# An attention and mixture-of-experts block in float32: weight loads and stores on ScalarE's queue, a row buffer of its own for the last batch, and a first tile table of eight

## The reference

```python
h = _layernorm(x) * (1 + ca) + sa
q, k, v = (h @ w + b, split into 16 heads)
scores = einsum('bhnd,bhmd->bhnm', q, k) * dmask      # gamma**(n-m), n >= m
ret = einsum('bhnm,bhmv->bhnv', scores, v)
x = x + ga * ((silu(h @ wg + bg) * groupnorm(ret)) @ wo + bo)
h = _layernorm(x) * (1 + cb) + sb
logits = h @ gate_kernel                              # 8 experts, the best 2, softmax over the 2
inter = silu(h @ w0[e]) * (h @ w1[e])                 # 256 -> 512
x = x + gb * sum over the 2 experts (weight * inter @ wo[e])
```

## Time and profile before

| | us |
|---|---|
| median of the 3 timed executions (422.52 to 423.67) | 422.94 |
| the profiled execution, device time | 424.81 |
| its span, from the first to the last instruction | 423.1 |
| first part, until PE turns the first routed rows | about 172 |
| tiles 0 to 8 | about 78 |
| tiles 9 to 38 and the last writes | about 173 |

### The profile page before, as it was taken

One profiled execution on the slowest core, in us unless ns is written; L12 is line 12 of the kernel. 1 busy time (PEld: TensorE's weight loads), 2 busy tenths in 40 slices (PEclk: granted clock), 3 DMA queues, 4 the chain that ended last, 5 costly groups with the idle time before them and its releaser, 6 DMA issues.

```text
span 423.1 us, 11448 instructions
## 1 busy us (share of the span) xinstructions
PE 373.8 (88%) x3889; PEld 278.0 (66%) x3890; DVE 257.2 (61%) x726; ACT 171.5 (41%) x262; POOL 229.5 (54%) x172
## 2 busy tenths in 40 slices
PE   3995899999889859887799899999999999999990
PEld 3464657776666537654476468888888888888870
DVE  6368317836833658673265566777777777777740
ACT  3514145463444311221331145555555555555530
POOL 3202520563754253617256457787777778777751
PEclk9998589999968988999699999999999999999997
DMA  6819007007900884217229844433333433433322
GB/s 226 273 34 317 4 24 279 28 2 258 323 24 3 282 294 119 52 52 252 53 42 285 245 84 75 78 75 75 75 75 75 75 75 75 75 75 76 51 25 25
DMA packets 32322, 49.05 MB, mean 116 GB/s; under 512 B 3198, under 2 KB 18972, under 8 KB 32284
## 3 DMA queue, kind: packets, MB, share of 16 engines
q1 hardware_dynamic: 23656, 34.60, 27.4%
q0 software_dynamic: 8176, 13.65, 14.6%
q10 hardware_dynamic: 452, 0.28, 0.2%
HBM read 30.35 MB, written 18.16 MB: 115 GB/s over the span
## 4 chain that ended last, share of the span: by engine, by line
PE 67%; issue 8%; DVE 8%; ACT 4%; DMA 4%; POOL 3%; SPq 2%; POOLq 0%; ACTq 0%; DVEq 0%
PE ps L1686 14%; PE ps L1391 9%; PE ps L1670 6%; PE ps L1667 6%; PE ps L1666 6%; PE ps L1678 3%; PE ps L1505 3%; PE ps L1657 3%; PE ps L1410 3%; PE ps L1444 2%; PE ps L1480 2%; DMA out_dram<-wg_s,qd 2%; POOL routed L591 2%; PE ps L1573 2%; PE ps L1465 1%
## 5 line engine op out<-in xcount | busy, mean ns | idle before, releaser
L623 POOL TENSOR_TENSOR w_lo<-we,w_hi 128x1024 fp32r<-128x1024 f32 x30 | 74.7, 2490 | 20.7 <-ACT w_hi L807 20.5
L1686 PE MATMUL ps<-we,qeo 128*128 x312 | 77.7, 393 | 6.6 <-ACT qeo L792 6.2
L1686 PEld LDWEIGHTS ps<-we,qeo 128*128 128x128 f32 x312 | 58.2, 193 | 25.1 <-issue 17.7
L633 POOL DMA_INDIRECT out_dram<-wg_s,qd x30 | 47.1, 1570 | 38.8 <-issue 15.8
L792 ACT COPY qeo<-ps 128x512 f32<-128x512 f32 x39 | 22.9, 586 | 105.1 <-PE ps L1678 105.1
L591 POOL DMA_INDIRECT routed<-h,idx x32 | 33.0, 1031 | 20.1 <-DVE idx L1131 11.2
L1292 DVE TENSOR_TENSOR w_halves<-we,w_halves 128x1024 fp32r<-128x1024 f32 x30 | 36.8, 1226 | 7.6 <-ACT w_halves L807 7.6
L1657 PE MATMUL ps<-we,xn 128*128 x72 | 36.5, 632 | 0.8 <-issue 0.8
L1272 DVE SCALAR_TENSOR_TENSOR sm<-sm,ps 128x512 f32<-128x512 f32 x39 | 26.5, 679 | 12.7 <-ACT sm L797 12.7
L1264 DVE CAST rT_halves<-ps 128x256 fp32r<-128x256 f32 x30 | 12.7, 424 | 33.2 <-PE ps L1573 33.2
L807 ACT CAST w_hi<-we 128x1024 fp32r x30 | 31.6, 1053 | 0.0
(11 more groups left out here) (228 smaller groups left out, 725.2 us busy)
## 6 DMA issues: line engine op xcount, KB each, us to landing
rowbuf<-routed SPq DMA_DIRECT2D x39, 260.5 KB, 2.9
we<-in_ffn_w_kernel_dram SPq DMA_DIRECT2D x16, 512.0 KB
we<-in_ffn_wo_kernel_dram SPq DMA_DIRECT2D x8, 512.0 KB
routed<-z SPq DMA_DIRECT2D x9, 260.5 KB, 3.9
xs<-in_attn_x_dram SPq DMA_DIRECT2D x4, 512.0 KB, 11.7
out_dram<-xs SPq DMA_DIRECT2D x4, 512.0 KB, 3.1
we<-in_wmod_dram SPq DMA_DIRECT2D x1, 1024.0 KB, 10.0
sbcb<-gsc_dram SPq DMA_DIRECT2D x4, 256.0 KB, 5.8
```

The costliest lines, as they stand in the source:

```text
L623: g.tensor_tensor(w_lo[1], expert_up(e, 1), w_hi[1].bitcast(F32), ALU.subtract)\
L633: g.indirect_dma_start(out, bass.IndirectOffsetOnAxis(ap=meta[s % 4][:, TOK - D:TOK - D + 1].bitcast(I32), axis=0), ey[s % 2], None, compu ...
L1686: last = mm(down_ps, eit[s % 2][:, k, :], weights(e, 2 * FT * F + k * D, D), start=k == 0, stop=k == KF - 1)
```

## The change

1. `load_expert` moves from SP to ACT. Experts 0 and 1 are issued after `keys(0, 1)`. For b = 1 to 3, expert 2b is issued after `queries(b, 0)` and expert 2b + 1 after `keys(b, 0)`. They no longer wait for `pv_done`.
2. `store_x` moves from SP to ACT, behind `features(b + 1)`, and for batch 3 behind step 2.
3. Batch 3 gets a row buffer of its own, `h2_last`, in the memory of `vx` and the first 36 columns of `z`. `second_normed(3)` and the fill of gb lose their wait for the scatters. The high halves of w0 lie in `vx` too, so ACT waits for all scatters before it writes those of tile `EARLY`.
4. `EARLY` goes from 9 to 8. `turn_h2(3)`, the router, `rank` and the second table come one step sooner on PE, DVE, ACT and POOL.
5. In batch 3, `counts(0)` on PE comes behind the projection k1. On DVE `tiles_before(0)` comes behind `group_stats` and `tile_columns(0)` ahead of `gated`.

```diff
-EARLY = 9
+EARLY = 8
...
+        h2_last = nc.alloc_sbuf_tensor_at("h2_last", [P, NC, ROW], F32, offset=offset["vx"])
+        h2 = [h2_first, h2_first, h2_first, h2_last]
...
-                load_expert(2 * b)
-                load_expert(2 * b + 1)
...
                 if i == 1:
-                    store_x(B - 2, x2_out)
                     sp.wait_ge(h2_ready, B - 1)
                     load_sbcb(B - 1)
-                if i == 3:
-                    store_x(B - 1, x2_last)
-                if i == 4:
                     fill_gb(B - 1)
-                if i == 7:
+                if i == 6:
...
                 queries(b, 0)
+                if b == B - 1:
+                    act.wait_ge(gb_out, 16)
+                if b:
+                    load_expert(2 * b)
...
                 keys(b, 0)
+                if b:
+                    load_expert(2 * b + 1)
                 keys(b, 1)
+                if b == 0:
+                    load_expert(0)
+                    load_expert(1)
...
                 act.wait_ge(shift2, b + 1)
-                if b:
+                if 0 < b < B - 1:
                     act.wait_ge(scattered, SCATTERS * b)
...
                     act.wait_ge(we_in, 16 * 3 * E)
+                    act.wait_ge(scattered, SCATTERS * B)
...
             second_normed(b)
-            act_step(2, 2)
             h2_features(b, [0])
-            act_step(3, 3, between=lambda: h2_features(b, [1]))
+            act_step(2, 2, between=lambda: h2_features(b, [1]))
+            store_x(b)
...
                     if last:
                         tiles_of_experts(0)
-                        tiles_before(0)
                     group_stats(p)
+                    if last:
+                        tiles_before(0)
...
+                if last:
+                    tile_columns(0)
                 if p >= 0:
                     gated(p)
                 fr.wait()
-                if last:
-                    tile_columns(0)
                 states(b)
...
-            pe_step(2, 2)
-            pe_step(3, 3, between=lambda: turn_h2(b, [0]), before_second=lambda: turn_h2(b, [1]),
+            pe_step(2, 2, between=lambda: turn_h2(b, [0]), before_second=lambda: turn_h2(b, [1]),
                     before_down=lambda: router(b))
-            pe_step(4, 4, before_second=lambda: rank(b))
-            pe_step(5, 5, between=lambda: counts(1))
-            pe_step(6, 6, between=lambda: firsts(1))
-            pe_step(7, 7, between=lambda: fold(1))
+            pe_step(3, 3, before_second=lambda: rank(b))
+            pe_step(4, 4, between=lambda: counts(1))
+            pe_step(5, 5, between=lambda: firsts(1))
+            pe_step(6, 6, between=lambda: fold(1))
```

More of the change, by code:

```diff
@@ L412, in _ @@
             load_ga(1)
-            def store_x(b, done_sem):
-                wait(sp, tail.drains(b, "wo23"))
-                sp.dma_start(out_v[b], xs[:, b * NC:(b + 1) * NC, :]).then_inc(done_sem, 16)
             def fill_gb(b):
-                if b:
+                if b == B - 1:
+                    sp.wait_ge(pv_done, SETS * B)
+                elif b:
                     sp.wait_ge(scattered, SCATTERS * b)
-                sp.dma_start(h2[:, 0, GB:ROW], gb_dram[b].partition_broadcast(P)).then_inc(gb_rows, 16)
-            for b in range(B):
+                sp.dma_start(h2[b][:, 0, GB:ROW], gb_dram[b].partition_broadcast(P)).then_inc(gb_rows, 16)
+            for b in range(1, B):
                 p = b - 1
[L427 to L431, removed]
-                    sp.wait_ge(gb_out, 16)
-                load_expert(2 * b)
-                load_expert(2 * b + 1)
[L435 to L445, removed]
+                sp.wait_ge(pv_done, SETS * b)
+                if b + 1 < B:
+                    sp.wait_ge(x1_ready, b)
+                    load_ga(b + 1)
+                if p >= 1:
+                    sp.wait_ge(h2_ready, p)
+                    load_sbcb(p)
+                if p == 0:
+                    sp.wait_ge(gb_out, 16)
+                fill_gb(p)
             def load_rows(i, s):
@@ L591, in scatter @@
                         g.indirect_dma_start(routed, bass.IndirectOffsetOnAxis(ap=idx[:, k, t:t + 1], axis=0),
-                                             h2[:, t, :], None).then_inc(scattered, 16)
+                                             h2[b][:, t, :], None).then_inc(scattered, 16)
             pool.sem_inc(added_ok, 4)
@@ L740, in gb_copies, with load_expert, store_x @@
                 act.wait_ge(gb_rows, 16 * (b + 1))
-                a.copy(h2[:, 1:NC, GB:ROW], h2[:, 0:1, GB:ROW].broadcast_to([P, NC - 1, D])).then_inc(gb_copied, 1)
+                if b == B - 1:
+                    act.wait_ge(prod_ready, FT * B)
+                a.copy(h2[b][:, 1:NC, GB:ROW], h2[b][:, 0:1, GB:ROW].broadcast_to([P, NC - 1, D])).then_inc(gb_copied, 1)
+            def load_expert(e):
+                for o, w, k, n in we_v:
+                    act.dma_start(we[:, e, o:o + k * n].rearrange("p (k n) -> p k n", k=k),
+                                  w[e].rearrange("(k p) n -> p k n", p=P)).then_inc(we_in, 16)
+            def store_x(b):
+                wait(act, tail.drains(b, "wo23"))
+                act.dma_start(out_v[b], xs[:, b * NC:(b + 1) * NC, :]).then_inc(x2_last if b == B - 1 else x2_out, 16)
             def top_tanh(b):
@@ L1334, in _ @@
             dve_step(2, 2, hidden_made=True)
-            dve_step(3, 3)
-            hidden(3, 3)
+            hidden(2, 2)
             take_logits(b)
@@ L1344, in _ @@
             tiles_of_experts(1)
+            dve_step(4, 4)
+            tiles_before(1)
             dve_step(5, 5)
-            tiles_before(1)
-            dve_step(6, 6)
             tile_columns(1)
-            dve_step(7, 7, between=lambda: table_rows(1))
+            dve_step(6, 6, between=lambda: table_rows(1))
+            dve_step(7, 7)
             run_steps(dve, dve_step, first=8)
```

39 lines of the change are left out of this document (19 added, 20 removed).

## The result

| | before | changed |
|---|---|---|
| executions beside each other, median (range), us | 423.07 (422.52 to 423.67) | 403.91 (402.78 to 409.48) |
| profiled execution, time / span, us | 424.81 / 423.1 | 404.24 / 402.5 |

The ratio is 0.954 (95% interval 0.951 to 0.957). The changed kernel run again on another chip gave 405.99 us (403.23 to 408.31) beside 420.97 (416.59 to 423.37) for the kernel before, a ratio of 0.970 (0.963 to 0.978); ratios compare the executions near each kernel's fastest, in which the core shows the higher clock.

A forecast was written before the change was run, and what follows sets the result against it. PE's pauses before 260 us, for ACT's copy and for code blocks queued behind expert weights, were taken as the bound to win. Gains of 7.7 + 1.2 + 4.8 + 3.2 + 3.8 = 20.7 us gave 402.5 us (range 397.5 to 412.5).

## What to carry to other kernels

A bulk load that nobody needs soon belongs where PE runs through few new instructions, since its traffic can hold back code. Here an earlier time went together with another queue. Issued by SP at nearly the same times, the load brought no long pause at the old places either; that the total is then as good is not shown. Before a late step is moved up by one tile, follow the whole chain behind it and price its landings too. Here additions, scatters and a row's load in one chain made eight early tiles dearer than nine, and nine with half of the template stores behind the next row's load was the fastest version (400.86 us). And see what VectorE does while GpSimd runs a long operation: moving that operation moved the collision twice.

## What was unexpected of the hardware

- An instruction block's packet may pass within full DMA queues, or PE may stand still 2.7 to 4.4 us for it. A kernel with such a meeting ranged from 405.9 to 421.2 us on one chip, which fits but was not traced execution by execution.
- A VectorE operation of 0.17 us took 1.8 beside a GpSimd operation on two SBUF operands, and ended with it; FIND_INDEX8 did not.
- The granted clock stood at 0.50 after batch 0 in some profiles and at 1.00 in others of nearly the same kernel, once at 0.50 with no pause with "issue" in the states. It is worth 2.5 us here. What decides it is open.
